# Experts' gelu from the scalar engine twice, and two weight parts per expert split by the vector engine

## The reference

```python
logits = jnp.einsum('bld,ed->ble', x, gate_weight)
kth_val = jnp.sort(logits.reshape(-1))[expert_k - 1]
gates = logits * (logits >= kth_val).astype(x.dtype)
h = jax.nn.gelu(jnp.einsum('bld,ehd->bleh', x, w1) + b1, approximate=True)
y = jnp.einsum('bleh,edh->blde', h, w2) + b2.T[None, None]
out = jnp.einsum('blde,ble->bld', y, gates)
```

## Time and profile before

| | |
|---|---|
| median of 3 runs | 1125.18 us (1121.58 to 1126.65) |
| the profiled execution's own time | 1126.08 us |
| its span in the trace | 1124.3 us |
| PE busy | 991.4 us, 88% |
| PE weight loads busy | 917.6 us, 82% |
| DVE busy | 660.9 us, 59% |
| ACT busy | 478.9 us, 43% |
| POOL busy | 255.7 us, 23% |
| mean granted clock of PE | 0.951 |

### The profile page before, as it was taken

How to read it: one execution, slowest core, us unless ns; L and a number is a source line. 1 busy time by engine, 2 the same in 40 slices (tenths; PEclk the granted TensorE clock), 3 DMA queues, 4 the chain that set the end, 5 groups by cost and what they waited for, 6 DMA issues and landing times.

```text
span 1124.3 us, 18908 instructions
## 1 busy us (share of the span) xinstructions
PE 991.4 (88%) x7314; PEld 917.6 (82%) x7314; DVE 660.9 (59%) x1389; ACT 478.9 (43%) x1351; POOL 255.7 (23%) x214
## 2 busy tenths in 40 slices
PE   5779999998588689999987889899999999999998
PEld 5668888777566668787866788899999999999998
DVE  4765254544898654244454587864857575858553
ACT  3446363652767255454552412323333333333231
POOL 0233030321032112121241201240414141414111
PEclk9899999998999789999997689899999999999999
DMA  6120000001021100000011010100202020200001
GB/s 246 75 113 1 1 2 1 2 1 39 0 75 38 38 1 2 1 1 1 2 39 38 10 66 1 45 32 1 76 1 76 1 75 1 75 1 1 1 3 42
DMA packets 8636, 34.48 MB, mean 31 GB/s; under 512 B 610, under 2 KB 5090, under 8 KB 5220
## 3 DMA queue, kind: packets, MB, share of 16 engines
q1 hardware_dynamic: 8548, 33.28, 8.2%
HBM read 32.06 MB, written 1.22 MB: 30 GB/s over the span
## 4 chain that ended last, share of the span: by engine, by line
PE 34%; issue 33%; DVE 16%; POOL 9%; ACT 6%; DMA 1%; POOLq 0%; SPq 0%; DVEq 0%; ACTq 0%
PE D L477 16%; POOL wslot L426 5%; PE S L477 4%; ACT probs L887 4%; PE O L631 3%; POOL h L320 3%; PE O L477 2%; DVE probsT L1142 2%; PE T L523 2%; PE O L725 2%; PE T L615 2%; DVE hid L1151 1%; DVE xc L1079 1%; PE T L513 1%; DVE negmax L1125 1%
## 5 line engine op out<-in xcount | busy, mean ns | idle before, releaser
L477 PE MATMUL O<-hid,wslot 128*128 128x300 f32 (+1 forms) x1536 | 220.5, 302 | 10.2 <-DVE work L1359 10.2
L477 PEld LDWEIGHTS O<-hid,wslot 128*128 128x128 f32 x1536 | 212.5, 189 | 12.6 <-DVE hid L1342 12.6
L477 PE MATMUL D<-xn,wslot 128*128 128x300 f32 (+3 forms) x1248 | 205.8, 313 | 6.3 <-ACT work L1003 6.2
L1340 DVE CAST hid<-work 128x300 fp32r<-128x300 f32 (+1 forms) x256 | 127.6, 498 | 135.9 <-ACT work L1003 135.2
L477 PE MATMUL S<-xn,wslot 128*128 128x300 f32 (+3 forms) x1248 | 199.6, 309 | 0.0
L477 PEld LDWEIGHTS D<-xn,wslot 128*128 128x128 f32 x1248 | 186.2, 194 | 9.6 <-ACT work L1003 6.4
L477 PEld LDWEIGHTS S<-xn,wslot 128*128 128x128 f32 x1248 | 184.8, 193 | 0.6
L1003 ACT ACTIVATE work<-D,prm 128x300 f32<-128x300 f32 (+1 forms) x128 | 64.3, 509 | 262.2 <-PE D L477 258.4
L1342 DVE TENSOR_TENSOR hid<-work,hid 128x300 fp32r<-128x300 f32 (+1 forms) x256 | 159.3, 622 | 8.8
L444 POOL TENSOR_TENSOR probs<-probs,rsum 111x444 f32<-111x444 f32 (+1 forms) x88 | 79.7, 905 | 319.2 <-DVE rsum L1134 319.2
L887 ACT ACTIVATE probs<-S,negmax 111x111 f32<-111x111 f32 (+1 forms) x240 | 81.0, 361 | 110.7 <-DVE negmax L1125 110.7
(11 more groups left out here) (150 smaller groups left out, 1241.7 us busy)
## 6 DMA issues: line engine op xcount, KB each, us to landing
raw<-in_moe SPq DMA_DIRECT2D x16, 1024.0 KB, 4.8
raw<-in_attn SPq DMA_DIRECT2D x8, 1024.0 KB, 4.8
work<-in_x SPq DMA_DIRECT2D x2, 1008.0 KB, 8.4
raw<-in_ffn SPq DMA_DIRECT2D x1, 1024.0 KB, 5.8
w2f<-in_ffn SPq DMA_DIRECT2D x1, 1024.0 KB, 7.8
raw<-in_x SPq DMA_DIRECT2D x1, 1008.0 KB, 6.8
out<-h SPq DMA_DIRECT2D x3, 300.0 KB, 2.9
raw<-in_w_lin SPq DMA_DIRECT2D x1, 768.0 KB, 4.5
```

Source lines behind the costliest of these rows:

```text
L477: mm = pe.matmul(psum, a, b, start=(first and k == 0), stop=(k == 3 * n - 1))
L1340: nc.vector.tensor_copy(high, moe_g(s)[:, 0:w]).then_inc(m_high, 1)
```

## The change

Per step of the experts, ACT now takes the same gelu twice from the PSUM bank: into the work buffer as before, and at once into the high part in `hid` (the output type does the rounding). DVE's copy L1340 goes away; its subtraction stays (`moe_low`). PE may reuse the bank only when the second gelu is done (`m_high` in place of `m_gelu`). The pieces of experts 2 to 7 are no longer subtracted by POOL but by DVE, in four quarters of 128x512: w1 of the next expert in c = 0 ahead of steps 4 to 7, w2 in c = 2 ahead of steps 0 to 3. Expert 1's two stay on POOL.

```diff
+        LATE_W = FIRST_W + 14
         def piece_split(i):
+            if i >= LATE_W:
+                return (dve_split, i - LATE_W + 1)
             return (start_split, i + 1) if i < NSTART else (pool_split, i - NSTART + 1 - past(i))
...
+        def moe_hid(s, k):
+            j, m, w = s // KH, s % KH, MCHUNKS[s // KH % NC][1]
+            return hid[:, j % 2, k, m * CW:m * CW + w]
...
             for e in range(1, E):
                 for c in range(NC):
-                    if c == 0 and e + 1 < E:
-                        for i in (2, 3):
-                            split(FIRST_W + W_MOE + 2 * e + i)
...
                     if s >= 4:
-                        pe.wait_ge(m_gelu, s - 3)
+                        pe.wait_ge(m_high, s - 3)
...
                 nc.scalar.activation(moe_g(s)[:, 0:w], BH[s % 4][:, 0:w], ACT.Gelu_apprx_tanh,
-                                     bias=prm[:, S_B1M + e * KH + m:S_B1M + e * KH + m + 1]).then_inc(m_gelu, 1)
+                                     bias=bias).then_inc(m_gelu, 1)
+                if s // KH >= 2:
+                    act.wait_ge(m2_mm, KD * (s // KH - 1))
+                nc.scalar.activation(moe_hid(s, 0), BH[s % 4][:, 0:w], ACT.Gelu_apprx_tanh,
+                                     bias=bias).then_inc(m_high, 1)
...
-            def moe_split(s):
-                c, m = s // KH % NC, s % KH
-                w = MCHUNKS[c][1]
-                j = s // KH
+            def moe_low(s):
+                w = MCHUNKS[s // KH % NC][1]
                 dve.wait_ge(m_gelu, s + 1)
-                if j >= 2:
-                    dve.wait_ge(m2_mm, KD * (j - 1))
-                high, low = (hid[:, j % 2, k, m * CW:m * CW + w] for k in range(2))
-                nc.vector.tensor_copy(high, moe_g(s)[:, 0:w]).then_inc(m_high, 1)
                 dve.wait_ge(m_high, s + 1)
-                nc.vector.tensor_tensor(low, moe_g(s)[:, 0:w], high.bitcast(F32), ALU.subtract).then_inc(m_hid, 1)
+                nc.vector.tensor_tensor(moe_hid(s, 1), moe_g(s)[:, 0:w], moe_hid(s, 0).bitcast(F32),
+                                        ALU.subtract).then_inc(m_hid, 1)
...
+            def low_quarter(i, k):
+                dve.wait_ge(high_ready, i + 1 - past(i))
+                high, low = piece_place(i)
+                sl = slice(k * PIECE // SPLITS, (k + 1) * PIECE // SPLITS)
+                nc.vector.tensor_tensor(low[:, sl], piece_raw(i)[:, sl], high.bitcast(F32)[:, sl],
+                                        ALU.subtract).then_inc(dve_split if k == SPLITS - 1 else dve_part, 1)
...
-                moe_split(s)
+                if n >= NC and n + NC < E * NC:
+                    e, c = steps[n]
+                    if c == 0 and m >= KH - SPLITS:
+                        low_quarter(FIRST_W + W_MOE + 2 * e + 2, m - (KH - SPLITS))
+                    if c == 2 and m < SPLITS:
+                        low_quarter(FIRST_W + W_MOE + 2 * e + 3, m)
+                moe_low(s)
```

More of the change, by code:

```diff
@@ L146, in vit_tower @@
         pool_split = sem("pool_split")
+        dve_split = sem("dve_split")
+        dve_part = sem("dve_part")
         dve_line = sem("dve_line")
@@ L1002, in _ @@
                     act.wait_ge(m_hid, s - 3)
+                bias = prm[:, S_B1M + e * KH + m:S_B1M + e * KH + m + 1]
                 nc.scalar.activation(moe_g(s)[:, 0:w], BH[s % 4][:, 0:w], ACT.Gelu_apprx_tanh,
-                                     bias=prm[:, S_B1M + e * KH + m:S_B1M + e * KH + m + 1]).then_inc(m_gelu, 1)
+                                     bias=bias).then_inc(m_gelu, 1)
[3 more added lines that the diff above has]
+                                     bias=bias).then_inc(m_high, 1)
                 if c == 1 and m == KH - 1 and e >= 1:
```

## The result

| | before | changed |
|---|---|---|
| median, 20 runs each | 1125.08 us | 1130.24 us (1119.22 to 1133.07) |
| ratio, 95% interval | | 1.0042 [1.0027, 1.0058] |
| profiled execution's time / span | 1126.08 / 1124.3 | 1131.45 / 1129.7 |

The change makes the kernel 0.4% slower. The forecast was 1122.8, 0.2% faster: the time lies inside the range, but the sign is wrong. First the page of the changed kernel: busy times, and PE's granted clock in 40 slices.

A forecast was written before the change was run, and what follows sets the result against it. PE was taken to bound the kernel, so only its few idle stretches could be won or lengthened. The terms 0.4 - 0.7 - 2.4 - 4.5 + 2.1 + 9.0 - 6.3 = -2.4 us gave 1122.8 from the median 1125.18; range 1117 to 1131.

The forecast's parts named there:

- c = 0: Experts 2 to 6: ACT's high part and second gelus delay the eviction, +0.4 us five times, +2.1.
- c = 2: Experts 1 to 6: PE's eviction waits go with POOL's two subtractions, -6.3 us; bounds 0 and -6.3.
- the price of c = 1: Experts 1 to 6: eight gelus delay the gate copy PE waits for, +1.5 us six times, +9.0; bounds 0 and 2.5 each.
- chunk 4: Search still on: without POOL holding DVE, PE's 5.11 us wait shrinks, -4.5 us; bounds -1.5 and -5.
- a failure of the gains: Partial failure of the gain side, which set the range's upper end at 1131.
- Chunk 0: At the first bank wait, one gelu interval more, +0.4 us.
- Chunks 1, 2, 3 and 4: DVE loses copies: -0.7 us in the first, -1.2 each in the next two, -4.5 in the last.
- the cover of 0.28 us: Plain chunk: PE's slack left after the eviction comes 0.04 us later; price 0.
- Expert 3's four chunks: The profile after should show them longer by about 0.9 us in all.
- Rival 1: Expert chunks: two gelus of one bank follow at 0.51 us each, ACT paces; +17 us, 1140; chance 0.14.
- Rival 2: Chunk 1: the 9.7 us wait's count comes up to 4.4 us sooner; -3.7 more, 1119; chance 0.14.
- Rival 3: Quarters leave DVE as late in c = 2 and chunk 4 as POOL did; +9.3 us, 1132; chance 0.07.

The follow-up runs named there:

- experiment 1: The changed kernel with ACT making w2's high part behind the gate copies of c = 1, no longer ahead of step 4: 1109.7 us, ratio 0.9864.
- experiment 5: The changed kernel with PE doing 11 unused matmuls where it waits for the gate copy: 1120.46 us, ratio 0.9959.
- experiment 2: The kernel before with one unused ACT copy of 1776 columns ahead of the gate copies of c = 1, experts 1 to 6: 1138.16 us, ratio 1.0121.
- experiments 2 and 3: The second of the pair: the changed kernel with all pieces left to POOL, so only the second gelu replaces DVE's copy: 1127.44 us, ratio 1.0022.
- experiment 4: The changed kernel with one gelu and DVE's copy as before, so only the quarters on DVE: 1123.90 us, ratio 0.9997.
- experiment 10: The changed kernel with both ACT high parts moved later and expert 1's pieces also in quarters on DVE: 1091.33 us, ratio 0.9708.

## Why the prediction was wrong

**The step that failed** is the price of c = 1, "+1.5 us, six times, +9.0. Bounds: 0 if PE is not held there, 2.5 if ACT is paced by latency". The mechanism, the place and the length of the wait were right: 1.54 us for 1.5, six times. What failed is that the price of a wait of PE was taken to be its length, with no term for the clock; the upper bound of 2.5 each had none either. The chunks of that term grew by 20.6 us: 9.7 for the six waits, near the 9.0 forecast, and on top of it 11 us of half clock (6.3 in chunk 5, three times 1.55): with the wait away, c = 1 and chunk 5 are 21.3 us shorter than in the changed kernel, where the six waits explain only 9.3 (experiment 1); with the wait filled, 10 us less (experiment 5); with the wait put into the kernel before, 13 more than before, net of the 7.6 won back at c = 2 (experiment 2). The profile had the warning. Behind the 5.11 us wait of chunk 4 I read half clock and used it in that term, and did not ask the same of the waits that the change would bring. The measured time lies inside the stated range only because its upper end, 1131, was set for a failure of the gains, which did not come: that is luck.

That may also be why the changed kernel's own runs scatter: the fastest, 1119.22, has a mean granted clock of 0.956, the slowest, 1133.07, 0.944, the profiled one 0.947. This fits a number of costly waits that differs from run to run; only the profiled run was looked at in its rows. It isn't the only source of scatter: PE's last matmuls ahead of the first bank wait start at 608.44 us in the profiled kernel before and at 605.44 in that of experiment 2, whose code is the same up to there.

**Chunk 0**, +0.4 forecast, was -2.8. The later start of 0.35 is there, but the router ran at another clock. It is the second place where the sum had no term for the clock, of opposite sign. Without both, 5.5 - 11.0 + 3.1 = -2.4 us is left of the difference. That this is exactly the sum that was forecast is luck in part: c = 0 and c = 1 cost 1.6 more, and c = 2 gave 1.3 more.

**Right, point by point.** Chunks 1, 2, 3 and 4 came within 0.1 us: DVE free of copies no longer paces the search, and PE's waits in chunk 4 were 1.15 and 0.70 (forecast 1.05, 0.1, 1.0). A plain chunk is 13.06 long in both kernels, so the cover of 0.28 us held. The gelus start 0.395 apart also when two read the same bank and one writes fp32r. c = 2 gave 7.6 instead of 6.3: a chunk lost 1.2 us before, and only 1.01 of it is in the listed wait. The reason given, that POOL's subtractions are gone, is one of two: the later start of PE behind the gate spread takes the wait away just as well (experiments 2 and 3), so the two terms were not independent. c = 0 cost 3.0 instead of 2.1 (whose own working, 0.39 five times, gives 2.0). Expert 3's four chunks grew by 2.8 instead of 0.9, of which 1.6 is half clock.

**The rivals.** Rival 1 (ACT the pacer) did not occur; the Trainium skill's budget of about 0.3 us per ACTIVATE plus 0.83 ns an element (ScalarE: Activation LUTs, Rules for kernel authors), 0.55 us by estimate, is near the 0.5 us that one gelu lasts, and far from the 0.395 at which they follow, which is what decides a sequence of them. Rival 2 (chunk 1 opens up) did not occur: PE waited 9.2 us there. Rival 3 did not occur, but experiment 4 is what it describes: with the copy still on DVE the quarters leave it as late at c = 2 as POOL did. None of the three was the way it went; a fourth, half clock behind a new wait, was missing from the list.

The Trainium skill (TensorE: Matmul & The Clock Gate, HAM oscillation) says that idle gaps of PE can put it back to half clock, and that the cost is paid behind the gap. The trace agrees in kind: it is the term that was missing. It does not agree in size: the page speaks of longer gaps than these, and by it none of the waits at the gate spread would have cost clock; the gaps that did it here are 1.5 us long, among small matmuls.

## What to carry to other kernels

A wait of a busy TensorE costs its length and perhaps a stretch at half clock behind it: look in busy time by stretch for what the clock did behind waits of that length and in such surroundings, and give the sum a term for it even where it may turn out zero. When work is added to an in-order engine, look for what stands right behind it in that engine's list (here the gate copies behind eight gelus and a weight copy) and move the work that has time, rather than counting busy shares: the same change with two pieces of ACT's work moved is 2% faster than the kernel before, and 3% with POOL out of the way. And an engine that holds another for a whole instruction (POOL's 4.7 us against a copy of 0.3) is worth freeing only if the engine freed has room for what it takes over.

## What was not expected of the hardware

- Half clock behind a wait of 1.50 to 1.54 us, in some places and not in others (chunk 5 in two of three kernels that have the wait; of experts 2 to 6 three, three and two), never behind 0.77 us. What decides it in one place was not found. Length alone does not: experiment 4 has PE waits of up to 1.43 us between large matmuls, and experiment 10 has one of 1.94 us for a count, all at a clock of 1.00 during and behind them:

```profile
829.31 6.69 PE L484 MATMUL O<-hid,wslot 128*128 128x294 f32 x48 [1.43 <-DVE work L1367]
...
637.24 0.38 PE L753 MATMUL T<-count,mean_w 128*128 128x1 f32 x2 [1.94 <-DVE probsT L1312]
```

- Eleven unused matmuls in each of six waits made the kernel 10 us faster, and an unused copy of 0.35 us on ACT ahead of a clock change made the kernel before 2.4 us faster.
- In a row of back-to-back gelus the listed duration creeps up while the interval stays near 0.395 us, as these two rows of the changed kernel's c = 0, expert 3, show (the first and the last of one run of them):

```profile
824.28 0.49 ACT L1011 ACTIVATE work<-D,prm 128x300 f32<-128x300 f32 x1
...
829.39 0.60 ACT L1015 ACTIVATE hid<-S,prm 128x300 fp32r<-128x300 f32 x1
```
